# Two gathered tiles in one VectorE multiply, with one signal a pair, in the edge stages of a graph-attention kernel

## The chip, the cores and the metric

The kernel is one program on one core of a Trainium2 chip. The metric is the device time of one launch in microseconds (us). TensorE (PE), VectorE (DVE), ScalarE (ACT), GpSimd (POOL) and SyncE (SP) each run their own list of instructions and wait for one another through semaphores.

## The reference, cut to what matters

A node matrix x (6250 x 256) goes through two graph-attention layers, a mixing block and a mixture of experts. The change lies in the attention layers. There are 106,250 edges, sorted by their target node `dst`, and 8 heads of 32 columns:

```python
xp = (x @ W).reshape(-1, Hh, C)
alpha = leaky_relu(a_src[src] + a_dst[dst] + a_edge, 0.2)
m = segment_max(alpha, dst)
ex = exp(alpha - m[dst])
denom = segment_sum(ex, dst)
alpha = ex / (denom[dst] + 1e-16)
msg = xp[src] * alpha[:, :, None]
out = segment_sum(msg, dst)
```

## The kernel before, in words

The edges are cut into 832 tiles of 128 edges (one edge per partition), and these into 52 groups of GT = 16 tiles. `edges()` (line 591) runs once for each of the two layers, one after the other; each run is called an edge stage here. What the engines do for group g, tile k:

- **POOL** (`gather`, line 710): before tile k of group g+2 is fetched into `rows[q]`, it waits until the message of tile k of group g is made, which frees that slot (`s["msg"]`, line 715; the semaphore starts at 32). Then one indirect DMA (L717) fetches 128 rows of 1104 bytes.
- **DVE** (`step`, line 874): `message(g, q, k)` (L758) multiplies the 256 columns of a tile's rows by the 8 probabilities of each edge, which lie in PSUM (`ps_pr[q]`), writes `msg[:, k % 8]` and adds 1 to `s["msg"]`. It needs a free slot of 8: `total` of tile k-8. Between the messages of group g stand the steps of the softmax of group g+1 and the one-hot matrices: `one_hots` r=3 of group g+1 after message 1; r=0 of group g+2 after message 5; `leaky` (L777 to L782) after 6; `highest` (L788) after 7; `less_highest` (L793 to L796) after 8; `one_hots` r=1 after 9; `running` (L801) after 10; `whole` (L807 to L810) after 11; `inverse` (L814) after 12; `probability` (L821) after 13; `one_hots` r=2 after 14. In layer 0 `keys_centred` (L826) stands after message 10 and `keys_scales` (L831 to L835) after message 15; in layer 1 `mixed` (L847, L849) stands after message 15.
- `one_hots` r (L736/L737, then two L748) overwrites the one-hots of four tiles of group g, so that r=0 waits for `total` of tile 3, r=1 for that of tile 7 and r=2 for that of tile 11 (line 731).
- **PE** (`step`, line 1146): `total(k)` (L1101) waits for message k and for a free PSUM buffer of three, and multiplies message k by its one-hot matrix (four matmul records a tile). `scores` (L1074, L1083) r=3 of group g+1 follow total 2, r=0, 1, 2 of group g+2 follow totals 9, 10, 15; `turn_alpha` (L1090) follows total 6 and `turn_prob` (L1094) total 13. Layer 0 adds `key_sums` after total 4 and `keys` (L1110) after total 8, layer 1 `turn_squares` after total 0 and `mix` (L1139, L1142) after total 8.
- **ACT** (`window`, line 950): L955 and L956 take the sums of tile k out of PSUM and free the buffer for total k+3. In layer 0 `block_squares` (L993 to L998) follows window 11; it makes k2s, which `keys_scales` on DVE waits for. At each group's start ACT loads 16 registers.

The order on each engine is written out by hand; a loop body holds two groups (q = 0 and 1).

## Time and profile before

| | us |
|---|---|
| three runs | 3894.82, 3909.32, 3885.41; median 3894.82 |
| profiled execution, span from first to last instruction | 3896.2 |
| edge stage of layer 0, from its first message | 1533.4 |
| edge stage of layer 1, from its first message | 1448.4 |

The profiled execution's span, 3896.2 us, lies within the three runs and 1.4 us above their median. The four rows are told apart by where they come from: the first by timing, the others by the hardware profiler. In a row of the timeline the first number is the start, the second the time busy, "xN" how many instructions are merged, and the bracket the idle time of the engine before it with what ended it. A PE row says when PE took up an instruction, with a modelled end; when its semaphore arrived elsewhere is seen from those who waited.

### The profile page before, as it was taken

The page shows a single profiled execution, that of the slowest core. Times are in us where ns is not written, and L with a number is a line of the kernel's source. Part 1 is how long each engine was busy: PE and PEld are TensorE (multiplying, and loading weights), DVE is VectorE, ACT ScalarE, POOL GpSimd, SP SyncE. Part 2 cuts the span into 40 slices and gives each one's busy share as a digit, 9 for nine tenths or more (in the row PEclk, how much of TensorE's full clock was granted, in tenths as well). Part 3 has the DMA queues.
Part 4 walks back from the last instruction along what each step waited for, and adds up shares of the span by engine and source line. Part 5 has one row for each costly group of instructions (what it writes and reads, how often), then busy time and mean ns, then how long its engine had stood idle before and what let it go on. Part 6 is the DMA issues. An engine that isn't in the chain of part 4 may idle for free. (4 is left out here: it accounts for less than half of the span.)

```text
span 3896.2 us, 76131 instructions
## 1 busy us (share of the span) xinstructions
PE 2654.0 (68%) x15613; PEld 2243.8 (58%) x15614; DVE 2154.7 (55%) x6066; ACT 1173.1 (30%) x4747; POOL 2020.7 (52%) x2269
## 2 busy tenths in 40 slices
PE   6466677677676666684666666666666666659988
PEld 4355555556565555563555555555555556548877
DVE  6355555555554555561555555555555556675655
ACT  3133333333332333342222222222222223442222
POOL 3555455545455454436455555555555554635665
PEclk8677676776677777787677767777777767779999
DMA  9533343433333433314444444444444443454443
GB/s 252 144 112 110 109 122 111 115 112 113 107 111 110 116 111 107 108 52 125 114 118 129 117 127 121 118 131 117 131 115 127 124 116 94 143 151 149 152 119 97
DMA packets 282186, 473.15 MB, mean 121 GB/s; under 512 B 69124, under 2 KB 191644, under 8 KB 282116
## 3 DMA queue, kind: packets, MB, share of 16 engines
q0 software_dynamic: 96912, 288.68, 26.8%
q1 hardware_dynamic: 120884, 137.12, 12.0%
q10 hardware_dynamic: 64320, 46.56, 3.8%
q8 instruction: 27, 0.44, 0.0%
q14 instruction: 43, 0.35, 0.0%
HBM read 398.47 MB, written 75.78 MB: 122 GB/s over the span
## 5 line engine op out<-in xcount | busy, mean ns | idle before, releaser
L717 POOL DMA_INDIRECT e_rows<-table,e_idx x1664 | 1585.7, 953 | 1469.8 <-DVE e_msg L758 1006.6
L1101 PE MATMUL e_ps_sum<-e_hot,e_msg 128*128 128x129 f32 x6656 | 1456.5, 369 | 955.6 <-ACT parts L956 479.6
L1101 PEld LDWEIGHTS e_ps_sum<-e_hot,e_msg 128*128 128x128 f32 x6656 | 1209.5, 261 | 1142.1 <-ACT parts L956 622.2
L955 ACT ACTIVATE acc<-e_ps_sum 128x256 f32 x1664 | 640.5, 385 | 2094.7 <-remote 936.3
L737 DVE TENSOR_TENSOR e_hot<-e_ps_pr,rel 128x512 f32<-128x512 f32 x416 | 286.4, 689 | 932.4 <-PE e_ps_sum L1101 494.8
L758 DVE TENSOR_TENSOR e_msg<-e_rows,e_ps_pr 128x256 f32<-128x256 f32 x1664 | 655.3, 414 | 82.0 <-issue 9.9
L956 ACT ACTIVATE parts<-e_ps_sum 128x4 f32 (+1 forms) x1664 | 279.5, 168 | 0.0
L1083 PE MATMUL e_ps_al<-e_dst_score,e_hotT 128*128 x3328 | 249.0, 181 | 43.7 <-issue 42.4
L1083 PEld LDWEIGHTS e_ps_al<-e_dst_score,e_hotT 128*128 128x128 bf16 x3328 | 223.4, 104 | 87.3 <-issue 45.4
L748 DVE TENSOR_SCALAR e_hotT<-e_relb,pcolf 128x512 bf16<-128x512 bf16 x416 | 149.9, 360 | 52.2 <-remote 36.3
L2295 ACT ACTIVATE x_h<-x,eb 128x128 f32<-128x128 f32 x216 | 67.7, 364 | 271.4 <-PE x L2369 232.6
L748 DVE TENSOR_SCALAR e_hotT<-e_relb,pfar 128x512 bf16<-128x512 bf16 x416 | 147.2, 354 | 0.0
L788 DVE TENSOR_TENSOR_SCAN e_peak<-e_mark,e_ps_al 128x128 f32<-128x128 bf16 x104 | 43.7, 420 | 179.2 <-PE e_ps_al L1090 90.0
L2390 PE MATMUL x<-acc,x_h 128*128 x432 | 123.0, 408 | 18.9 <-DVE x_h L2325 13.7
L2369 PEld LDWEIGHTS x<-x_h,x_w 128*128 128x128 f32 x864 | 109.3, 194 | 28.4 <-ACT x_h L2295 15.7
L2369 PE MATMUL x<-x_h,x_w 128*128 128x128 f32 x864 | 122.2, 285 | 4.7 <-ACT x_h L2295 3.6
L2369 PE MATMUL x<-x_yT,x_w 128*128 128x128 f32 x864 | 116.7, 279 | 0.0
L2336 DVE TENSOR_TENSOR x_raw<-x,eb3b 128x256 f32<-128x256 f32 x108 | 45.9, 425 | 114.8 <-PE x L2390 93.8
L1110 PE MATMUL e_ps_a<-wkq,e_xT 128*128 128x512 f32 x200 | 108.0, 668 | 0.0
L2369 PEld LDWEIGHTS x<-x_yT,x_w 128*128 128x128 f32 x864 | 107.4, 195 | 0.1
L1118 PE MATMUL e_ps_b<-e_xc,e_k2r 128*128 128x256 f32 x200 | 101.8, 607 | 0.6 <-ACT e_k L1003 0.3
L814 DVE RECIPROCAL e_seg<-e_ps_pr 128x128 f32<-128x128 f32 x104 | 98.9, 951 | 0.1
(370 smaller groups left out, 3380.9 us busy)
## 6 DMA issues: line engine op xcount, KB each, us to landing
e_relb<-rel_rows SPq DMA_DIRECT2D x104, 512.0 KB
e_rows<-table,e_idx POOLq DMA_INDIRECT x1664
e_eattr<-in_edge_b SPq DMA_DIRECT2D x104, 128.0 KB
e_xT<-turned_x ACTq DMA_DIRECT2D x100, 128.0 KB
e_xr<-in_x ACTq DMA_DIRECT2D x100, 128.0 KB
node<-l_row SPq DMA_DIRECT2D x25, 512.0 KB, 3.1
table<-t_row SPq DMA_DIRECT2D x25, 276.0 KB
table<-j_row SPq DMA_DIRECT2D x25, 276.0 KB, 2.5
```

Source lines behind the costliest of these rows:

```text
L717: nc.gpsimd.indirect_dma_start(out=rows[q][:, k, :], out_offset=None, in_=table[0:NP], in_offset=bass.IndirectOffsetOnAxis(ap=idx[:, q, k: ...
L737: nc.vector.tensor_tensor(hot[:, q, 4 * r:4 * r + 4, 0:P], iota[c].unsqueeze(1).broadcast_to((P, 4, P)), rel[:, bass.ds(g * GT + 4 * r, 4) ...
L748: op = nc.vector.tensor_scalar(hotT[:, r % 2, far], relb[:, q, 4 * r:4 * r + 4, :], number[:, 0:1], None, ALU.is_equal)
L758: nc.vector.tensor_tensor(msg[:, k % RM, :].rearrange("p (h c) -> p h c", c=C), rows[q][:, k, 0:F].rearrange("p (h c) -> p h c", c=C), ps_ ...
L955: nc.scalar.activation(acc[:, :, bass.ds(at[k], P)], ps_sum[(k + q) % 3][:, :, 0:P], ACT.Copy).then_inc(s["window"], 1)
L956: nc.scalar.activation(parts[:, bass.ds(g * GT + k, 1)].rearrange("p t a b -> p (t a) b"), ps_sum[(k + q) % 3][:, :, 0:P + 1:P], ACT.Copy) ...
L1083: op = nc.tensor.matmul(parts_al[:, m, :], hotT[:, r % 2, far, k, :], pieces[:, bass.ds(b + far, 1), :].rearrange("p a c -> p (a c)"), sta ...
L1101: op = nc.tensor.matmul(ps_sum[(k + q) % 3][:, a, 0:WIN], msg[:, k % RM, a * P:a * P + P], hot[:, q, k, :], start=(a == 0), stop=True, ski ...
L1110: op = nc.tensor.matmul(ps_a[:], xT[:, q, a, :], wkq[:, a, :], start=(a == 0), stop=(a == 1))
L1118: nc.tensor.matmul(ps_b[:, a * F:a * F + F], k2r[:, a * P:a * P + P], xc[:], start=False, stop=False, skip_group_check=True)
L2369: op = nc.tensor.matmul(ps[k % 2][:, a * P:a * P + P], w[:, k % 2, m, h, a * P:a * P + P], of[:, h, :], start=(h == 0), stop=(h == 1))
L2390: op = nc.tensor.matmul(ps_3[k % 2][:, 0:F], h2[:, h, :], ew[:, 2, bass.ds(e, 1), h, :].rearrange("p e f -> p (e f)"), start=(h == 0), sto ...
```

## The change

DVE makes the messages of two tiles with one instruction (`messages(g, q, k)` for even k) of 128 x 512 elements, which waits for total k-7 and adds 1 to `s["msg"]` for the pair. POOL waits for the pair of its tile before each gather, PE before each even total. The softmax steps are placed between pairs: `one_hots` r=3 after pair 0, r=0 after pair 4, `leaky` after pair 6, `highest` and `less_highest` after pair 8, then after pair 10 `keys_centred` (layer 0), `one_hots` r=1 and `running`, after pair 12 `whole`, `inverse` and `probability`, and after pair 14 `keys_scales` (layer 0) or `mixed` (layer 1) and then `one_hots` r=2.

```diff
                 for k in range(GT):
-                    pool.wait_ge(s["msg"], 16 * g + k + 1)
+                    pool.wait_ge(s["msg"], 8 * g + k // 2 + 1)
                     pool.nop(nofuse=True)
...
-            def message(g, q, k):
+            def messages(g, q, k):
                 if k == 0:
                     vec.wait_ge(s["probT"], g + 1)
-                vec.wait_ge(s["sum"], 16 * g + 16 + k - RM + 1)
+                vec.wait_ge(s["sum"], 16 * g + 16 + k - RM + 2)
                 nc.vector.tensor_tensor(
-                    msg[:, k % RM, :].rearrange("p (h c) -> p h c", c=C),
-                    rows[q][:, k, 0:F].rearrange("p (h c) -> p h c", c=C),
-                    ps_pr[q][:, H * k:H * k + H].unsqueeze(2).broadcast_to((P, H, C)), ALU.mult).then_inc(s["msg"], 1)
+                    msg[:, k % RM:k % RM + 2, :].rearrange("p k (h c) -> p k h c", c=C),
+                    rows[q][:, k:k + 2, 0:F].rearrange("p k (h c) -> p k h c", c=C),
+                    ps_pr[q][:, H * k:H * k + 2 * H].rearrange("p (k h) -> p k h", k=2).unsqueeze(3).broadcast_to((P, 2, H, C)),
+                    ALU.mult).then_inc(s["msg"], 1)
...
-                for k in range(GT):
-                    message(g, q, k)
...
+                for k in range(0, GT, 2):
+                    messages(g, q, k)
+                    if softmax and k == 0:
                         one_hots(n, p, 3, None, q)
+                    if ahead and k == 4:
                         one_hots(g + 2, q, 0, i + 1, q)
                     if softmax and k == 6:
                         leaky(n, p, i if p == 1 else i + 1, more=ahead)
+                    if softmax and k == 8:
                         highest(n, p, i if p == 1 else i + 1)
                         less_highest(n, p)
+                    if block_too and layer == 0 and k == 10:
+                        keys_centred(g)
+                    if ahead and k == 10:
                         one_hots(g + 2, q, 1, i + 1, q)
                     if softmax and k == 10:
                         running(n, p)
+                    if softmax and k == 12:
                         whole(n, p)
                         inverse(p)
                         probability(n, p)
+                    if block_too and layer == 0 and k == 14:
+                        keys_scales(g)
+                    if block_too and layer == 1 and k == 14:
+                        mixed(g, q, i)
                     if ahead and k == 14:
                         one_hots(g + 2, q, 2, i + 1, q)
-            vec.sem_inc(s["msg"], 32)
+            vec.sem_inc(s["msg"], 16)
...
             def total(g, q, k):
-                pe.wait_ge(s["msg"], 16 * g + 32 + k + 1)
+                if k % 2 == 0:
+                    pe.wait_ge(s["msg"], 8 * g + 16 + k // 2 + 1)
```

## Rows read from the trace of the kernel before

**Rows 1.** Busy time by stage: window, busy us (instructions) by engine, PE clock, DMA share, GB/s
```profile
176.65:1710.06 1533.41, 1062.24 (x6050) 886.11 (x6049) 824.13 (x2452) 500.43 (x2214) 764.22 (x800) 0.72 0.39 110
1865.15:3313.57 1448.42, 948.48 (x5745) 825.00 (x5745) 819.69 (x2351) 391.45 (x1764) 760.47 (x800) 0.72 0.43 120
```

**Rows 2.** Groups by line, 1870 to 3310 us: busy, mean ns, idle before, releasers
```profile
L717 POOL DMA_INDIRECT e_rows<-table,e_idx x797 | 757.6, 951 | 663.5 <-DVE e_msg L758 460.0 <-issue 203.5
...
L758 DVE TENSOR_TENSOR e_msg<-e_rows,e_ps_pr 128x256 f32<-128x256 f32 x826 | 325.4, 414 | 39.8 <-remote 4.9 <-PE e_ps_sum L1101 2.1 <-issue 0.2
...
L737 DVE TENSOR_TENSOR e_hot<-e_ps_pr,rel 128x512 f32<-128x512 f32 x200 | 137.6, 688 | 496.9 <-remote 349.5 <-PE e_ps_sum L1101 147.4
```

**Rows 3.** Timeline of POOL in one group of layer 1
```profile
2492.46 0.94 POOL L717 DMA_INDIRECT e_rows<-table,e_idx  x1 [4.19 <-DVE e_msg L758]
2494.03 0.94 POOL L717 DMA_INDIRECT e_rows<-table,e_idx  x1 [0.62 <-issue]
...
2500.29 0.95 POOL L717 DMA_INDIRECT e_rows<-table,e_idx  x1 [0.30 <-issue]
2505.34 0.95 POOL L717 DMA_INDIRECT e_rows<-table,e_idx  x1 [4.11 <-DVE e_msg L758]
2507.06 0.95 POOL L717 DMA_INDIRECT e_rows<-table,e_idx  x1 [0.77 <-issue]
...
2516.07 0.95 POOL L717 DMA_INDIRECT e_rows<-table,e_idx  x1 [0.30 <-issue]
2521.28 0.95 POOL L717 DMA_INDIRECT e_rows<-table,e_idx  x1 [4.25 <-DVE e_msg L758]
```

**Rows 4.** Timeline of DVE in the same group
```profile
2492.82 0.75 DVE L758 TENSOR_TENSOR e_msg<-e_rows,e_ps_pr 128x256 f32<-128x256 f32 x2
...
2503.02 0.69 DVE L737 TENSOR_TENSOR e_hot<-e_ps_pr,rel 128x512 f32<-128x512 f32 x1 [6.62 <-PE e_ps_sum L1101]
...
2504.15 0.41 DVE L758 TENSOR_TENSOR e_msg<-e_rows,e_ps_pr 128x256 f32<-128x256 f32 x1
...
2514.16 0.41 DVE L758 TENSOR_TENSOR e_msg<-e_rows,e_ps_pr 128x256 f32<-128x256 f32 x1
2518.95 0.69 DVE L737 TENSOR_TENSOR e_hot<-e_ps_pr,rel 128x512 f32<-128x512 f32 x1 [4.38 <-remote]
...
2520.09 0.41 DVE L758 TENSOR_TENSOR e_msg<-e_rows,e_ps_pr 128x256 f32<-128x256 f32 x1
...
2521.41 0.74 DVE L758 TENSOR_TENSOR e_msg<-e_rows,e_ps_pr 128x256 f32<-128x256 f32 x2
```

**Rows 5.** Timeline of PE in the same group: total 3 and total 11
```profile
2496.88 0.71 PE L1101 MATMUL e_ps_sum<-e_hot,e_msg 128*128 128x129 f32 x4
...
2513.14 0.71 PE L1101 MATMUL e_ps_sum<-e_hot,e_msg 128*128 128x129 f32 x4
```

**Rows 6.** Timeline of DVE at the end of a group of layer 0
```profile
1005.67 0.41 DVE L758 TENSOR_TENSOR e_msg<-e_rows,e_ps_pr 128x256 f32<-128x256 f32 x1
1009.59 0.69 DVE L737 TENSOR_TENSOR e_hot<-e_ps_pr,rel 128x512 f32<-128x512 f32 x1 [3.51 <-PE e_ps_sum L1101]
...
1011.05 0.15 DVE L831 TENSOR_SCALAR e_k2s<-e_k2s 128x1 f32<-128x1 f32 x1
...
1012.18 0.75 DVE L758 TENSOR_TENSOR e_msg<-e_rows,e_ps_pr 128x256 f32<-128x256 f32 x2 [0.44 <-issue]
```

**Rows 7.** The same stretch on POOL (last gather of the burst) and on ACT
```profile
1007.56 0.95 POOL L717 DMA_INDIRECT e_rows<-table,e_idx  x1 [0.30 <-issue]
...
1010.21 0.20 ACT L993 ACTIVATION_READ_ACCUMULATOR e_k<-e_kq 128x1 f32 x1
```

**Rows 8.** Timeline of DVE in another group of layer 0
```profile
1302.70 0.42 DVE L788 TENSOR_TENSOR_SCAN e_peak<-e_mark,e_ps_al 128x128 f32<-128x128 bf16 x1 [3.71 <-PE e_ps_al L1090]
...
1306.99 0.69 DVE L826 TENSOR_TENSOR e_kq<-e_ps_a,bkq 128x512 f32<-128x512 f32 x1 [0.71 <-PE e_ps_a L1110]
...
1314.63 0.75 DVE L758 TENSOR_TENSOR e_msg<-e_rows,e_ps_pr 128x256 f32<-128x256 f32 x2 [0.44 <-issue]
```

More of the change, by code:

```diff
@@ L877, in step @@
                 block_too = not isinstance(g, int) or g < NB
-                for k in range(GT):
-                    message(g, q, k)
-                    if block_too and layer == 0:
-                        if k == 10:
-                            keys_centred(g)
-                        if k == 15:
-                            keys_scales(g)
-                    if block_too and layer == 1 and k == 15:
-                        mixed(g, q, i)
-                    if softmax and k == 1:
+                for k in range(0, GT, 2):
+                    messages(g, q, k)
+                    if softmax and k == 0:
                         one_hots(n, p, 3, None, q)
-                    if ahead and k == 5:
+                    if ahead and k == 4:
                         one_hots(g + 2, q, 0, i + 1, q)
@@ L892, in step @@
                         leaky(n, p, i if p == 1 else i + 1, more=ahead)
-                    if softmax and k == 7:
+                    if softmax and k == 8:
                         highest(n, p, i if p == 1 else i + 1)
-                    if softmax and k == 8:
                         less_highest(n, p)
-                    if ahead and k == 9:
+                    if block_too and layer == 0 and k == 10:
+                        keys_centred(g)
+                    if ahead and k == 10:
                         one_hots(g + 2, q, 1, i + 1, q)
@@ L900, in step @@
                         running(n, p)
-                    if softmax and k == 11:
+                    if softmax and k == 12:
                         whole(n, p)
-                    if softmax and k == 12:
                         inverse(p)
-                    if softmax and k == 13:
                         probability(n, p)
+                    if block_too and layer == 0 and k == 14:
+                        keys_scales(g)
+                    if block_too and layer == 1 and k == 14:
+                        mixed(g, q, i)
                     if ahead and k == 14:
                         one_hots(g + 2, q, 2, i + 1, q)
-            vec.sem_inc(s["msg"], 32)
+            vec.sem_inc(s["msg"], 16)
             vec.wait_ge(s_on, 1)
```

## The prediction

> **What bounds the kernel now.** I read the busy time by stage first. The two edge stages take 1533 and 1448 of the span's 3896.2 us, 77%, and in neither is an engine busy all the time: over the second, PE is busy 948 us, DVE 820 and POOL 760 of 1448 [rows 1]. So something passes the turn from one engine to another. The groups by line say where DVE stands still: not before its messages (40 us idle before 826 of them) but before the one-hots, 497 us before 200 [rows 2]. They wait for totals 3, 7 or 11, that is, for PE.
>
> Then I laid the timelines of one group of layer 1 beside each other. POOL's gathers come in bursts 1.25 us apart: gather 15 of the group before at 2492.46, gathers 0 to 5 from 2494.03 to 2500.29, idle, gathers 6 to 14 from 2505.34 to 2516.07, idle, gather 15 at 2521.28 [rows 3]. The one-hots r=0 run at 2503.02, r=2 at 2518.95, both after more than 4 us of idle time [rows 4]. But PE took up the totals that these wait for much earlier: total 3 at 2496.88 with an end at 2497.59, total 11 at 2513.14 with an end at 2513.85 [rows 5]. The reports come 5.4 and 5.1 us after these ends, and each comes shortly after a burst has ended: the last gather of the first burst ends at 2501.24 and the report is there 1.78 us later, the last of the second at 2517.02 and the report 1.93 us later. I read it so: while a burst of gathers runs, what PE has finished is reported late, and a group is a ring: burst, report, one-hots, message, next burst. In layer 0 the same is seen at the group's end: gather 14 ends at 1008.51, one-hots r=2 start at 1009.59 [rows 6, 7], 1.0 us later with the wait itself taken off.
>
> **A pair's price.** No row has a message of 128x512. Two messages back to back take 0.75 us, 0.34 from start to start [rows 4]. The nearest rows of 512 elements with an operand in PSUM are L737 with 688 ns [rows 2] and L826 with 690 [rows 8]. I take 0.69: a pair signals 0.28 us later than one message (0.414) did, and frees DVE 0.06 us sooner than two did. Bounds: 0.41 us (no more than now for one) and 0.83 (twice 0.414). With 8 pairs that is 0.5 us of DVE's time a group, which in layer 1 lies in the idle time before L737 and is worth nothing by itself. Half of the signals fall away; I price that at nothing, since no row shows idle time that a signal makes (0.2 us "issue" before 826 messages [rows 2]); the bounds are 0 and 0.05 us a pair.
>
> **Layer 1, by POOL's ring.** From gather 15 to the next gather 15 there are 28.82 us: 1.57 to gather 0, 6.26 to gather 5, 5.05 to gather 6, 1.72 to gather 7, 9.01 to gather 14, 5.21 to gather 15 [rows 3].
> - After the first burst: report, one-hots r=0 (1.13 us, from L737 at 2503.02 to the message at 2504.15), message, 0.78 us until POOL starts. With a pair 5.05 becomes 5.33.
> - Gathers 6 to 15: gather 7 no longer waits for `leaky`, which stood between messages 6 and 7, and gather 15 no longer for the report of total 11, because pair 14 makes message 15 before the one-hots r=2. DVE makes pair 14 at about the time of message 14 now (2514.16), and gather 14 is due at 2505.34 + 8 x 1.25 = 2515.3, so nine intervals of 1.25 to 1.26 follow: 11.3 us in place of 1.72 + 9.01 + 5.21 = 15.94.
> - After gather 15 comes what came after gather 14: 0.95 for the gather, 1.93 until the report, 1.13 for the one-hots r=2, 0.69 for pair 0, 0.78 until POOL starts: 5.48 in place of 1.57. `mixed` (1.0 us between 2520.4 and 2521.41) now lies before the one-hots, in the idle time before the report.
> - Sum: 5.48 + 6.26 + 5.33 + 11.3 = 28.37, 0.45 less than 28.82. Over some 50 groups: **-22 us**.
>
> So message 15 and `mixed` leave the path (1.33 us), but the report then comes one gather later. What is late next is the report itself, as before. The slot of a message is no new bound: pair k needs total k-7 where messages k and k+1 needed k-8 and k-7, and before L758 there are only 40 us of idle time in the whole stage [rows 2]. The steps that now stand behind a pair and not behind one message (`leaky` by 0.28 us) are covered by the 4.38 us that DVE waits at L737 later in the group [rows 4]; without that cover they would cost 0.28 each.
>
> A page of the Trainium skill speaks against reading the pauses so: "SBUF — State Buffer", section "SBUF: two separate sides", says that engine ports and DMA ports are disjoint and that PE never waits for anyone. The pauses in this trace end with the bursts all the same. What the rule would make of the change is the third rival.
>
> **Layer 0.** From the end of message 14 to the next message 0 there are 6.10 us (1006.08 to 1012.18): 3.51 waiting for total 11, 1.13 one-hots r=2, 0.33 message 15, 0.69 `keys_scales`, 0.44 the loop [rows 6]. After the change the order is pair 14, `keys_scales`, one-hots r=2. `keys_scales` waits for k2s, which ACT ends at 1010.41, 0.9 us after the report [rows 7]. Two cases:
> - *Total 11 is still reported after the burst.* The burst now ends with gather 15. From the end of pair 14: 0.78 to gather 14, 1.25 to gather 15, 0.95 for it, 1.0 to the report: 4.0; then 0.9 for k2s, 0.69, 1.13, 0.44: 7.17. The one-hots r=1 now stand behind L826 and not in front of its wait of 0.71 us [rows 8], so pair 14 ends some 0.3 us later (1.13 less the wait and less two messages' savings). Together **+1.4 us a group**.
> - *Total 11 is reported earlier.* Pair 8 no longer waits behind `highest` (which waited 3.71 us for PE [rows 8]), so gathers 6 to 9 and then 10, 11 come earlier, and there is a hole of about 2 us before pair 12, because the one-hots r=1 and `running` stand between. Through this hole the reports can pass. Then nothing is waited for behind pair 14: 0.69 + 1.13 + 0.44 = 2.26 in place of 6.10, less the 0.3: **-3.5 us a group**. The group at 1302.70 shows what such a group is like: DVE runs from L788 to the next message 0 in 11.9 us with 0.71 of waiting for PE in it [rows 8].
> I take 4 groups in 10 as free and 6 as held, as the trace of before has both sorts: 0.4 x (-3.5) + 0.6 x 1.4 = -0.56 a group, **-28 us** over 50. The ends are all held (+70) and, since a group that ends sooner meets its own next burst (pairs 4 and 6 need totals 13 and 15), not more than -2 us a group when all are free (-100).
>
> **Sum.** -22 - 28 = -50 from the profiled execution's 3896.2: **3846 us**. Its span lies 1.4 us above the median of the runs, less than their spread of 24, so nothing is added for that.
>
> **The rivals.**
> 1. *All of layer 0 is held* (slower). Place: `keys_scales` and one-hots r=2 behind pair 14, both behind one late report that now also waits for gather 15. Price +1.4 a group; it decides from the point at which more than 8 groups in 10 are held (there 0.8 x 1.4 = 1.12 stands against 0.2 x 3.5 + 0.45 = 1.15). For it: the wait of 3.51 us and the k2s that comes after it [rows 6, 7]. Against: the hole. 3896 + 70 - 22 = 3944.
> 2. *The hole lets nearly all reports through.* 3896 - 100 - 22 = 3774. For it: [rows 8]. Against: more groups back to back mean fewer idle stretches of POOL, through which PE catches up.
> 3. *The pauses are PE's own* and stay where they are, whatever POOL does (the page's rule). Then layer 1 gains all that stood behind the report, 2.46 - 1.13 = 1.33 a group [rows 4], -66, and layer 0 has 0.9 + 0.69 + 1.13 + 0.44 + 3.51 = 6.67 for 6.10, +28: 3896 - 38 = 3858.
> 4. *Only the later signal is felt.* The gathers do not close up, and at the two places a group where POOL stands idle for a message it gets a pair 0.28 us later: 0.56 x 102 groups = +57: 3953; half of it if the slack between gathers absorbs one place.
>
> **Chances.** A measurement of this kernel tells about 1% from no change, 39 us: faster is below 3857, slower above 3933. My forecast 0.38, of which 0.23 faster and 0.15 the same (its own range is 3810 to 3885). Rival 1 0.22: 0.18 slower, 0.04 the same. Rival 2 0.17, faster. Rival 3 0.12: 0.05 faster, 0.07 the same. Rival 4 0.11: 0.07 slower, 0.04 the same. Together faster 0.45, the same 0.30, slower 0.25. The range takes in both outer rivals and a little beyond: 3765 to 3965, which leaves out 2 in 10.
>
> **What would show it.** Right: 832 messages of 128x512 at about 0.69 us; in layer 1 ten gathers in a row from gather 6 on, and the one-hots r=2 starting 1.9 us behind the end of gather 15; stretches of 28.4 us from message 0 to message 0; `mixed` ahead of the one-hots r=2 and not behind a wait; in layer 0 a mixture of groups in which L831 waits and groups in which it does not. Wrong: a report of total 11 during the burst in layer 1, or at the old place (rival 3); L831 behind a wait of 4 us in nearly every group of layer 0 (rival 1) or in none (rival 2); gathers as far apart as before (rival 4); a pair far from 0.69 us.

## The result and the profile after

The changed kernel takes 3923.93 us (median of 8 runs, 3917.49 to 3949.38) against 3894.42 for the kernel before (8 runs beside them): a ratio of 1.0074 with an interval of 1.0055 to 1.0092, 0.7% slower. I had forecast 3846. The profiled execution is the slowest of the eight (3949.38, span 3947.6), so what the profile shows as lost, 51 us against the span of 3896.2, is more than the 30 us between the medians; the sizes by stage below are those of that one execution.

The costliest groups of the page of the kernel after (line, engine, operation; busy, mean ns; idle time before them and what ended most of it):

```profile
L717 POOL DMA_INDIRECT e_rows<-table,e_idx x1664 | 1577.1, 948 | 1524.1 <-DVE e_msg L758 1041.2
...
L737 DVE TENSOR_TENSOR e_hot<-e_ps_pr,rel 128x512 f32<-128x512 f32 x416 | 285.6, 687 | 766.4 <-PE e_ps_sum L1099 444.2
L758 DVE TENSOR_TENSOR e_msg<-e_rows,e_ps_pr 128x512 f32<-128x512 f32 x832 | 556.1, 679 | 74.4 <-PE e_ps_pr L1091 53.8
```

A pair takes 679 ns; 0.69 was forecast. And busy time by stage, to be read against [rows 1]:

```profile
174.32:1703.54 1529.22, 1053.48 (x6050) 886.00 (x6049) 789.14 (x2036) 500.67 (x2214) 759.48 (x800) 0.74 0.39 110
1858.42:3361.21 1502.79, 914.75 (x5745) 804.47 (x5744) 788.93 (x1935) 394.65 (x1764) 756.55 (x800) 0.75 0.41 116
```

Layer 0 is 4.2 us shorter, layer 1 is 54.4 us longer, 1.09 us a group. DVE works 35 and 31 us less in them, and that bought next to nothing. The whole loss lies in layer 1.

**Layer 1.** First DVE at the end of one group (start, us busy, what it is, and in brackets the idle time before it and what ended it), from pair 14 on:

```profile
2499.25 0.68 DVE L758 TENSOR_TENSOR e_msg<-e_rows,e_ps_pr 128x512 f32<-128x512 f32 x1
2501.40 0.43 DVE L848 TENSOR_TENSOR e_base<-e_ps_b,e_xr 128x256 f32<-128x256 f32 x1 [1.47 <-remote]
...
2506.18 0.69 DVE L737 TENSOR_TENSOR e_hot<-e_ps_pr,rel 128x512 f32<-128x512 f32 x1 [3.70 <-remote]
...
2508.75 0.69 DVE L758 TENSOR_TENSOR e_msg<-e_rows,e_ps_pr 128x512 f32<-128x512 f32 x1 [1.35 <-PE e_ps_pr L1091]
```

POOL in the same stretch, gathers 6 and 15 of the burst, and gather 0 of the next group:

```profile
2491.52 0.94 POOL L717 DMA_INDIRECT e_rows<-table,e_idx  x1 [3.95 <-DVE e_msg L758]
...
2502.77 0.95 POOL L717 DMA_INDIRECT e_rows<-table,e_idx  x1 [0.30 <-issue]
2510.21 0.95 POOL L717 DMA_INDIRECT e_rows<-table,e_idx  x1 [6.50 <-DVE e_msg L758]
```

ACT's first window after the burst, and the PE work that follows it:

```profile
2505.81 0.38 ACT L952 ACTIVATE acc<-e_ps_sum 128x256 f32 x1 [10.02 <-remote]
```

```profile
2506.31 2.09 PE L1099 MATMUL e_ps_sum<-e_hot,e_msg 128*128 128x129 f32 x8 [3.92 <-ACT parts L953]
2508.19 0.42 PE L1091 MATMUL e_ps_pr<-ident,e_prob 128*128 128x128 f32 x1
```

The gathers went as forecast: 6 to 15 in a row from 2491.52 to 2502.77, 11.25 us (so in 39 of the 50 groups; in the others the burst has a wait in it and takes 12.1 to 16.8). What came behind didn't. The report comes 2.46 us after the end of gather 15 (2503.72 to 2506.18), where 1.93 was forecast. Then DVE stands idle for 1.35 us before pair 0. Such a wait of over 0.5 us before message 0 stood in 3 groups of this layer before and stands in 43 now. Pair 0 needs `turn_prob` (L1091), and PE comes to that only behind totals 12 and 13 (the eight matmuls of 2506.31), which had themselves waited for ACT to empty a PSUM buffer. ACT had itself stood idle for 10.02 us before its first window. So a late report does not hold up DVE alone. It leaves a backlog on ACT and PE, and that is worked off only after it.

Before, this backlog was smaller. ACT's window 9 and PE's last work before message 0, in the group of [rows 4]:

```profile
2515.01 0.39 ACT L955 ACTIVATE acc<-e_ps_sum 128x256 f32 x1 [5.34 <-PE e_ps_sum L1101]
```

```profile
2519.28 1.23 PE L1101 MATMUL e_ps_sum<-e_hot,e_msg 128*128 128x129 f32 x4 [3.06 <-ACT parts L956]
2520.30 0.42 PE L1094 MATMUL e_ps_pr<-ident,e_prob 128*128 128x128 f32 x1
```

Window 9 ran inside the burst, 2.0 us before its end at 2517.02, and freed the buffer for total 12. So one total (13) stood between the report and `turn_prob`, which PE took up 1.35 us behind the one-hots r=2. After, window 9 runs only with the report (2505.81), two totals stand there, and it is 2.01 us. Over the groups 10 to 43 it is one total in 33 of 34 before and two in 29 of 34 after.

One group can mislead, so here is the ring of the prediction over the groups 10 to 43 of layer 1, worked out from the starts of the gathers, one-hots and messages in the traces (mean us a group; e9 and e10 are two kernels of the experiments below). "Last gather" is the last of the second burst: 14 before and in e9, 15 after and in e10.

| stretch | forecast | before | after | e9 | e10 |
|---|---|---|---|---|---|
| gather 6 to the last gather | 11.3 | 11.06 | 11.99 | 10.74 | 11.26 |
| last gather to one-hots r=2 | 2.88 | 2.64 | 3.04 | 2.96 | 2.98 |
| one-hots r=2 to the next gather 0 | 2.60 | 3.83 | 3.78 | 4.29 | 4.55 |
| of this, to message or pair 0 | 1.13 | 2.63 | 2.32 | 3.09 | 3.09 |
| gather 0 to gather 5 | 6.26 | 6.57 | 6.82 | 6.89 | 6.87 |
| gather 5 to gather 6 | 5.33 | 4.47 | 3.96 | 5.80 | 6.11 |
| whole group | 28.37 | 28.57 | 29.59 | 30.67 | 31.77 |

In most groups of the kernel after, the third row is 4.03 and the fourth 2.56 (the middle values); the means are lower because in some groups the report is not late.

**Layer 0.** The end of a group, DVE: `keys_centred` (L827), pair 12 (1309.03), pair 14, `keys_scales` (L832), one-hots r=2, and the next one-hots r=0:

```profile
1306.73 0.69 DVE L827 TENSOR_TENSOR e_kq<-e_ps_a,bkq 128x512 f32<-128x512 f32 x1 [1.99 <-issue]
...
1309.03 0.69 DVE L758 TENSOR_TENSOR e_msg<-e_rows,e_ps_pr 128x512 f32<-128x512 f32 x1 [0.15 <-issue]
...
1311.88 0.68 DVE L758 TENSOR_TENSOR e_msg<-e_rows,e_ps_pr 128x512 f32<-128x512 f32 x1
1312.48 0.15 DVE L832 TENSOR_SCALAR e_k2s<-e_k2s 128x1 f32<-128x1 f32 x1
...
1313.29 0.69 DVE L737 TENSOR_TENSOR e_hot<-e_ps_pr,rel 128x512 f32<-128x512 f32 x1
...
1326.99 0.69 DVE L737 TENSOR_TENSOR e_hot<-e_ps_pr,rel 128x512 f32<-128x512 f32 x1 [9.37 <-PE e_ps_sum L1099]
```

Behind pair 14 nothing waits any more: the free case of the forecast. But 9.37 us are lost at the next one-hots. To see how common this is, the waits before all one-hots of layer 0, first of the kernel before (68 + 16 + 1 waits in 50 groups), then of the kernel after (47 + 3):

```profile
its engine sat idle before it (us, times) until:
  PE e_ps_sum L1101: 347.4, 68
  remote: 83.0, 16
```

```profile
  PE e_ps_sum L1099: 363.6, 47
  remote: 21.4, 3
```

Before, there were nearly two late reports a group; after, there is one. But the time fell only from 431 to 391 us. And `keys_centred` now waits, first before, then after:

```profile
L826 DVE TENSOR_TENSOR e_kq<-e_ps_a,bkq 128x512 f32<-128x512 f32 x50 | 34.6, 692 | 23.2 <-PE e_ps_a L1110 16.2 <-issue 6.1
```

```profile
L827 DVE TENSOR_TENSOR e_kq<-e_ps_a,bkq 128x512 f32<-128x512 f32 x50 | 34.6, 691 | 140.2 <-remote 84.0 <-PE e_ps_a L1108 34.0 <-issue 22.2
```

That is 117 us more, against 39 gained before the one-hots, 31 before the messages (40.8 to 9.6) and 35 less of DVE's own work: these nearly cancel, and the stage is 4.2 us shorter. By one-hots, the 34 waits at r=2 are all gone; the 50 at r=0 stay and grow from 316 to 385 us.

### The profile page after: what moved, and what is told of

It reads as the page before. It is cut to its first block and busy times, and to the rows that moved or that the text cites. A ratio compares the mean times of both kernels' runs of the same rounds, so it can differ in the third digit from the quotient of the medians.

```text
span 3947.6 us, 72835 instructions
## 1 busy us (share of the span) xinstructions
PE 2608.1 (66%) x15613; PEld 2219.3 (56%) x15614; DVE 2088.3 (53%) x5234; ACT 1176.0 (30%) x4747; POOL 2011.0 (51%) x2269
## 5 line engine op out<-in xcount | busy, mean ns | idle before, releaser
L1099 PE MATMUL e_ps_sum<-e_hot,e_msg 128*128 128x129 f32 x6656 | 1348.9, 355 | 904.6 <-ACT parts L953 407.4
L1099 PEld LDWEIGHTS e_ps_sum<-e_hot,e_msg 128*128 128x128 f32 x6656 | 1161.4, 255 | 1022.4 <-ACT parts L953 602.7
L758 DVE TENSOR_TENSOR e_msg<-e_rows,e_ps_pr 128x512 f32<-128x512 f32 x832 | 556.1, 679 | 74.4 <-PE e_ps_pr L1091 53.8
L1080 PE MATMUL e_ps_al<-e_dst_score,e_hotT 128*128 x3328 | 296.1, 183 | 158.2 <-DVE e_hotT L748 80.7
L1080 PEld LDWEIGHTS e_ps_al<-e_dst_score,e_hotT 128*128 128x128 bf16 x3328 | 240.8, 102 | 234.1 <-issue 178.0
L2388 PE MATMUL x<-acc,x_h 128*128 x432 | 121.6, 404 | 21.5 <-DVE x_h L2323 14.7
L827 DVE TENSOR_TENSOR e_kq<-e_ps_a,bkq 128x512 f32<-128x512 f32 x50 | 34.6, 691 | 140.2 <-remote 84.0
```

The source lines that it names most:

```text
L758: nc.vector.tensor_tensor(msg[:, k % RM:k % RM + 2, :].rearrange("p k (h c) -> p k h c", c=C), rows[q][:, k:k + 2, 0:F].rearrange("p k (h ...
L1080: op = nc.tensor.matmul(parts_al[:, m, :], hotT[:, r % 2, far, k, :], pieces[:, bass.ds(b + far, 1), :].rearrange("p a c -> p (a c)"), sta ...
L1099: op = nc.tensor.matmul(ps_sum[(k + q) % 3][:, a, 0:WIN], msg[:, k % RM, a * P:a * P + P], hot[:, q, k, :], start=(a == 0), stop=True, ski ...
L2388: op = nc.tensor.matmul(ps_3[k % 2][:, 0:F], h2[:, h, :], ew[:, 2, bass.ds(e, 1), h, :].rearrange("p e f -> p (e f)"), start=(h == 0), sto ...
```

## The experiments

The kernels ran in five jobs, each beside the kernel before. In four of them the kernel before took 2979 to 2982 us, not 3894, and in one 3940. This was not foreseen, and it decides what each run can tell; I call the first sort *prompt* and the second *late*, as on the chip of the prediction. All ratios are to the kernel before in the same job.

### The prompt chips: the change moves nothing there

**e1** lets gather 15 wait for the next pair 0, which takes it out of the burst:

```diff
-                    pool.wait_ge(s["msg"], 8 * g + k // 2 + 1)
+                    pool.wait_ge(s["msg"], 8 * g + k // 2 + (1 if k < 15 else 2))
```

> The changed kernel, but POOL holds gather 15 of each group back until pair 0 of the next group (its rows are free earlier), so that the second burst ends with gather 14 as before the change. Theory A (what PE has finished is reported only after a burst has ended, and the change costs because gather 15 joined the second burst): in layer 1 the one-hots r=2 come about 1.25 us earlier than in the changed kernel, the mean group falls from 29.6 by 0.5 to 1.2 us, and the time falls by 25 to 60 us, to 3865 to 3900. Rival B (the pair's first signal, 0.28 us later, costs): nothing changes in the ring but a gather moved, the time stays at 3910 to 3940. Rival C (the pauses are PE's own): the same as B, and the one-hots r=2 stay where they are.

**e2** brings `turn_prob` forward from behind total 13 to behind total 11:

```diff
-                    if softmax and k == 13:
+                    if softmax and k == 11:
```

> The changed kernel with turn_prob on PE after total 11 and not after total 13. In the changed kernel pair 0 of the next group starts 2.1 us after the one-hots r=2 in layer 1 and not 1.13, since it waits for the turned probabilities, which stand on PE behind total 13 and so behind window 10, that is behind the late report. Theory A (that wait is a term of its own on the path): pair 0 follows the one-hots at once, the group of layer 1 falls by 0.7 to 1.0 us, the time by 25 to 50 us, to 3875 to 3900. Rival D (POOL's ring and the report set the pace, the wait is covered by them): within 10 us of the changed kernel.

**e3** keeps the new order but makes two single messages with a signal each:

```diff
                 for k in range(0, GT, 2):
-                    messages(g, q, k)
+                    message(g, q, k)
+                    message(g, q, k + 1)
...
```

The waits of POOL and PE count by tile again, as in the kernel before.

> The changed kernel's order of steps, but with two single instructions and two signals in place of each pair (832 pairs become 1664 messages). Theory A (the order costs, since messages 14 and 15 are made before the late report, and the pair instruction is worth little): within 12 us of the changed kernel, 3912 to 3936. Rival B (the pair's late first signal costs 0.28 us at two places a group): 30 us or more faster than the changed kernel. A third view, that the pair instruction saves time on DVE's path: 15 us or more slower than the changed kernel.

**e4** has pairs in nearly the old order: `highest` behind pair 6, the one-hots r=1 behind pair 8, `whole` behind pair 10, and the one-hots r=2 ahead of pair 14, so that gathers 14 and 15 wait for the report:

```diff
                 for k in range(0, GT, 2):
+                    if ahead and k == 14:
+                        one_hots(g + 2, q, 2, i + 1, q)
                     messages(g, q, k)
...
                     if softmax and k == 6:
                         leaky(n, p, i if p == 1 else i + 1, more=ahead)
+                        highest(n, p, i if p == 1 else i + 1)
                     if softmax and k == 8:
-                        highest(n, p, i if p == 1 else i + 1)
                         less_highest(n, p)
+                    if ahead and k == 8:
+                        one_hots(g + 2, q, 1, i + 1, q)
...
                         running(n, p)
-                    if softmax and k == 12:
                         whole(n, p)
+                    if softmax and k == 12:
                         inverse(p)
...
-                    if ahead and k == 14:
-                        one_hots(g + 2, q, 2, i + 1, q)
```

> Pairs as in the changed kernel, but the steps stand as near to their old places as pairs allow: highest before pair 8, one-hots r=1 after pair 8 and before keys_centred, whole after pair 10, and one-hots r=2 before pair 14, so that gathers 14 and 15 both wait for the report of total 11. Theory A (the order around the report is what costs): the second burst ends with gather 13, the report comes 1.25 us earlier than before the change and about 2.5 us earlier than in the changed kernel, but two gathers then run in the next burst. The time is 3870 to 3905, near the kernel before. Rival B (the pair costs wherever it stands): 3925 or more.

Measured beside 2978.98 us before: e1 2978.49 (0.9990, interval 0.9975 to 1.0004), e2 2978.40 (0.9989, 0.9974 to 1.0003), e3 2974.55 (0.9988, 0.9973 to 1.0002), e4 2978.65 (0.9994, 0.9984 to 1.0004). All four theories missed, since the kernel before itself was another: to see why, **e5** is the kernel before and **e6** the kernel after, unchanged.

> The kernel before, unchanged, for its profile on a chip of the experiments, where it took 2979 us beside the first four kernels and not 3894. Theory A2 (on the chip of the two first profiles PE's reports come late while gathers run, on this chip they come at once, and then POOL's 1664 gathers 1.25 us apart bound the edge stages): 2970 to 2990 us, gathers 1.25 us apart with little idle time, the one-hots r=0 and r=2 within 1 us of the end of totals 3 and 11. Rival (this chip is faster in the instructions or transfers themselves): gathers, messages or matmuls are shorter than in the first profile. If the chip is of the first kind, 3880 to 3910 and the first profile again.

> The changed kernel, unchanged. Theory A2 (POOL's gathers bound the stages where the reports come at once, and the change moves no gather there): within 0.3% of the kernel before, if that takes 2979. Rival (the pair saves DVE's time on the path): 0.5% or more faster. If the kernel before takes 3894 here: 0.5 to 0.9% slower, as in the first result.

e5 2978.38 us (one execution); e6 2977.23 (0.9993, 0.9983 to 1.0003). The page of e5, the kernel before on a prompt chip:

```profile
L717 POOL DMA_INDIRECT e_rows<-table,e_idx x1664 | 1582.4, 951 | 561.0 <-issue 399.2
...
L758 DVE TENSOR_TENSOR e_msg<-e_rows,e_ps_pr 128x256 f32<-128x256 f32 x1664 | 653.5, 413 | 74.6 <-PE e_ps_sum L1101 10.3
L737 DVE TENSOR_TENSOR e_hot<-e_ps_pr,rel 128x512 f32<-128x512 f32 x416 | 285.1, 685 | 157.7 <-PE e_ps_sum L1101 152.4
```

One gather, one message and one set of one-hots last as long as on the late chip. What is gone is the waiting: the gathers have 561 us idle before them where they had 1470 on the page of before, most of it "issue", in other words POOL's own step from one gather to the next, and the one-hots wait 158 us. The timeline of POOL shows gathers 1.25 us apart all through a group, 16 of them in 20.02 us:

```profile
1979.56 0.94 POOL L717 DMA_INDIRECT e_rows<-table,e_idx  x1 [0.30 <-DVE e_msg L758]
...
1999.58 0.95 POOL L717 DMA_INDIRECT e_rows<-table,e_idx  x1 [0.30 <-issue]
```

A group takes 20.6 us there on average. So where reports are prompt, POOL's gathers are nearly all of a group's time, and what DVE does is hidden. **e7** and **e8** take that cover away: they leave out the gathers of the odd tiles, in the kernel before and in the kernel after (the output then lacks those rows' share; `leaky` waits for 8 landed gathers a group in place of 16).

```diff
+                    if k % 2 == 0:
                         nc.gpsimd.indirect_dma_start(
...
```

> The kernel before with the gathers of odd tiles left out (their rows stay zero), so that POOL has 8 gathers a group in place of 16. Theory A2: where the kernel before takes 2979, POOL no longer bounds and the next bound (the ring of DVE, PE and ACT) shows: a group falls from 20.4 us by 0.5 to 3 us. Where it takes 3894, the pauses before the one-hots shrink with the bursts, and the group falls from 28.6 and 30.2 us by 6 us or more. Rival (PE's late reports have nothing to do with gathers): where it takes 3894, the pauses stay as long as they were.

> The changed kernel with the same gathers left out. With POOL out of the way this shows what pairs and the new order are worth to DVE, PE and ACT alone. My estimate from the two profiles: 0.5 us a group less on DVE, against turn_prob's wait before pair 0 and the later scales, so within 1% of the half-gather version of the kernel before. Rival (the pair instruction is a gain that the gathers hide): 1.5% or more faster than that one. Rival (the order is a loss by itself): 1.5% or more slower.

e7 2802.41 us (0.9404, 0.9388 to 0.9419), e8 2814.76 (0.9445, 0.9429 to 0.9461): with POOL half idle the change costs 0.4%. By stage it isn't one effect but two. Over the groups 10 to 43 of layer 1 the messages 0 stand 18.73 us apart in e7 and the pairs 0 18.05 in e8, 0.68 less; in layer 0 19.06 and 19.91, 0.85 more. The one-hots in layer 0 (160 to 1120 us), e7 first:

```profile
L738 DVE TENSOR_TENSOR e_hot<-e_ps_pr,rel 128x512 f32<-128x512 f32 x199 | 136.2, 685 | 74.1 <-PE e_ps_sum L1103 74.1
```

```profile
L738 DVE TENSOR_TENSOR e_hot<-e_ps_pr,rel 128x512 f32<-128x512 f32 x192 | 131.5, 685 | 131.7 <-PE e_ps_sum L1101 125.7
```

In layer 1 the granted clock of TensorE is nearly the same in the two (0.93 and 0.94), and the kernel after gains there: DVE's time counts where POOL doesn't. In layer 0 it loses more, at the one-hots and at `keys_centred` (2.7 us of waiting in e7, 32.5 in e8), which both wait for PE. But the granted clock of layer 0 also differs, 0.98 in e7 and 0.88 in e8, and PE is busy for 854.72 and 902.81 us. How much of the 0.85 is the order and how much the slower PE, no run separates.

### Late reports rebuilt on a prompt chip

**e9** is the kernel before with late reports put in by hand: DVE's one-hots r=0 and r=2, and ACT's windows 2 and 9, also wait until gathers 0 to 5, or 0 to 14, of group g+2 have landed.

```diff
                     vec.wait_ge(s["sum"], 16 * g + 4 * r - 12)
+                    if r in (0, 2):
+                        vec.wait_ge(s[f"rows{q}"], 256 * i + 16 * (6 if r == 0 else 15))
...
+                    if k in (2, 9) and (not isinstance(g, int) or g + 2 < NG):
+                        act.wait_ge(s[f"rows{q}"], 256 * i + 256 + 16 * (6 if k == 2 else 15))
```

> The kernel before with the late reports rebuilt by hand: where the first profile showed them late, VectorE (one-hots r=0, r=2) and ScalarE (windows 2 and 9) wait until the data of the first 6 and the first 15 gathers of group g+2 have landed, which are the gathers of the two bursts. Nothing is left out. Theory A3 (a report that comes when the burst has ended is what made a group 28.6 us long, and nothing else of that chip is needed): a group of layer 1 takes 27.5 to 29.5 us, with two bursts and two idle stretches of POOL of about 4 us, and the time is 3700 to 3950 us. Rival (that chip is slow for another reason, this does not rebuild it): under 3400.

**e10** is the kernel after with the same waits; the second is for gathers 0 to 15, since gather 15 is part of its burst (16 for 15 in both lines).

> The changed kernel with the same waits; the second burst now has gather 15 in it, so that the second wait is for all 16 gathers of group g+2. Theory A3: the second report comes one gather (1.25 us) later, pair 0 then waits for turn_prob behind total 13 and window 10, and a group of layer 1 is 0.5 to 1.5 us longer than in the kernel before with the same waits; the time is 0.5 to 2.5% more than that one's. My old step (the ring without the turn_prob term): 0.4 us a group less than that one. Rival: no difference within 0.3%.

e9 4115.69 us (1.3813 of before), e10 4228.10 (1.4199), beside 2980.5. The rule was put in by hand, so that the report comes one gather later in e10 is assumed, not shown. What is shown is whether the kernel after gains elsewhere what this costs. It doesn't. The two edge stages, e9 and then e10:

```profile
155.29:1839.53 1684.24, 1049.78 (x6050) 858.96 (x6049) 830.58 (x2452) 503.95 (x2215) 763.74 (x806) 0.73 0.35 100
1972.37:3535.85 1563.48, 940.07 (x5743) 818.52 (x5742) 816.31 (x2351) 390.87 (x1764) 763.04 (x806) 0.72 0.40 112
```

```profile
153.35:1889.59 1736.24, 1043.27 (x6048) 861.52 (x6048) 796.38 (x2036) 504.31 (x2214) 763.51 (x806) 0.75 0.34 97
2021.20:3639.30 1618.10, 895.90 (x5743) 802.21 (x5742) 785.74 (x1935) 391.12 (x1764) 762.22 (x806) 0.72 0.38 108
```

Layer 1 grows by 54.6 us, as in the real pair (54.4). Layer 0 grows by 52, where the real pair lost nothing: here the rebuilt rule is too strict, as it holds the one-hots r=2 in every group. So e9 and e10 stand for layer 1 alone. Even there 54.6 beside 54.4 is in part chance: the profiled execution of the kernel after was 25 us above its median. And e9 holds ACT's window 9 until the report, which the real kernel before did not, so that two totals stand ahead of `turn_prob` in all of its groups. That makes the pair a clean test of the other half: what taking DVE's work away is worth once PE's backlog is the same. Message 0 behind the one-hots r=2, in e9 (message 15 and `mixed` between them) and in e10 (nothing between them):

```profile
2710.23 0.69 DVE L739 TENSOR_TENSOR e_hot<-e_ps_pr,rel 128x512 f32<-128x512 f32 x1 [4.46 <-issue]
...
2713.30 0.75 DVE L760 TENSOR_TENSOR e_msg<-e_rows,e_ps_pr 128x256 f32<-128x256 f32 x2 [0.55 <-PE e_ps_pr L1098]
```

```profile
2722.31 0.69 DVE L739 TENSOR_TENSOR e_hot<-e_ps_pr,rel 128x512 f32<-128x512 f32 x1 [4.81 <-DMA e_rows<-table,e_idx]
2725.38 0.69 DVE L760 TENSOR_TENSOR e_msg<-e_rows,e_ps_pr 128x512 f32<-128x512 f32 x1 [1.86 <-PE e_ps_pr L1095]
```

It is 3.07 us in both. The 1.33 us of DVE's work that the change took away stands in the second as idle time: `turn_prob` is what both wait for. The table above says where the 1.10 us between e9 and e10 arise: 0.52 in the burst, which has gather 15 more and a wait for `leaky` less; 0.26 between pair 0 and gather 0, and 0.31 up to gather 6, the two places at which POOL waits for a message and a pair signals later than one message did.

**e11** (e10 with `turn_prob` behind total 11, the edit of e2) and **e12** (e10 with gather 15 held back, the edit of e1, and the second wait for 15 gathers again) take the two suspects one at a time.

> As the changed kernel with late reports, with turn_prob after total 11 in place of 13, in front of the window that is late. Theory A3 (the wait of pair 0 for the turned probabilities is a term of its own): pair 0 follows the one-hots r=2 at once, 0.7 to 1.0 us a group less than the changed kernel with late reports, 70 to 100 us in all. Rival D (POOL's ring covers that wait): within 15 us of it.

> As the changed kernel with late reports, with gather 15 held back until pair 0 of the next group, and the second wait for 15 gathers as in the kernel before. Theory A3: the second report comes 1.25 us earlier, but gather 15 then leads the next burst and ends the first burst 1.25 us later, as before the change; a group is 0.2 to 0.9 us shorter than in the changed kernel with late reports. Rival B (the pair's later signal is the cost): no shorter.

e11 4215.72 us (1.4152), e12 4188.97 (1.4055). In e11 pair 0 no longer waits for `turn_prob` and starts 1.13 us behind the one-hots r=2 instead of 3.1, but the pair of tiles 2 and 3 then starts 4.7 us after pair 0 instead of 3.0: the one-hots r=3 ahead of it overwrite those of tiles 12 to 15, and so wait for total 15, the end of PE's backlog (2.8 us of idle time where e10 has 1.0). Of 1.9 us only 0.38 a group are kept in layer 1 (1599.05 for 1618.10), and layer 0 gives 0.25 of that back. The backlog is one piece, and the next wait behind it pays. In e12 layer 1 takes 1586.11: holding gather 15 back returns 0.64 of the 1.09 us a group. It isn't the kernel before in this place, though: gather 15 now waits for pair 0 and delays gather 0 by 1.25 us (5.80 us from the one-hots r=2), so that what the second burst gains is lost again, and what remains is gained in the next burst.

### A late chip

The next job met a late chip: 3940.13 us before (3928.47 to 3953.89). The three kernels that ran on it carry the rebuilt waits besides the chip's own late reports, so they are all longer, and they can be compared with one another only.

**e13** is e10 with the single messages of e3, **e14** e10 in the order of e4 (second wait for 14 gathers, the last before the report), **e15** e10 with the one-hots r=2 directly behind pair 14:

```diff
                     messages(g, q, k)
+                    if ahead and k == 14:
+                        one_hots(g + 2, q, 2, i + 1, q)
```

> The kernel after with the late reports rebuilt (e10), but each pair is again two single messages with a signal each; the order of the softmax steps is the new one. Theory (the new order costs: gather 15 joins the burst, the report is a gather later, and the backlog of PE and ScalarE behind it is bare; the pair itself costs next to nothing): within 0.5% of e10's 4228 us, so 4207 to 4249, and layer 1 again 1.0 to 1.2 us a group longer than in e9. Rival (the pair's later signal is what is felt, 0.28 us at two places a group): 0.56 x 102 = 57 us less than e10, 4171, and if the signal is all of the loss, e9's 4116.

> Pairs, but the order of before as far as pairs allow it: highest after pair 8, then the one-hots r=1, and the one-hots r=2 ahead of pair 14, so that gathers 14 and 15 wait for the report, as gather 15 did before; rebuilt late reports: the second one until gather 13 has landed (the last that doesn't depend on it). Theory (order costs, pair is free): the report comes one gather (1.25 us) earlier than in e9 and two earlier than in e10, but two gathers stand behind it instead of one: in layer 1 near e9, 4070 to 4160 us in all. Rival (the pair's signal is felt): as e10, 4200 or more.

> e10 with one line moved: the one-hots r=2 stand directly behind pair 14, ahead of keys_scales (layer 0) and mixed (layer 1). Theory for layer 0 (its loss of 1.06 us a group against e9 is made behind the report: keys_scales, 0.69 us, waits for k2s and holds up the one-hots r=2 and with them PE's first scores): 0.5 to 1 us a group less in layer 0, and nothing in layer 1, where pair 0 waits for probT anyway: 4175 to 4205 us. Rival (layer 0 too is bound by PE's and ScalarE's backlog behind the report): within 0.4% of e10, 4211 to 4245.

e13 4361.38 us (1.1059, 1.1015 to 1.1102), e14 4232.05 (1.0731, 1.0691 to 1.0772), e15 4341.23 (1.1017, 1.0974 to 1.1060). The times expected for them by the theories were worked out from prompt chips and all missed; e14 lies in its rival's range (4200 or more), which on this chip says nothing. The stages tell more. Layer 0 and layer 1 of e13, then of e14, then of e15:

```profile
174.62:1942.22 1767.60, 1065.20 (x6050) 882.79 (x6049) 824.19 (x2452) 515.86 (x2214) 758.03 (x800) 0.72 0.34 95
2097.11:3763.12 1666.01, 938.78 (x5745) 826.85 (x5744) 817.24 (x2351) 401.05 (x1763) 758.68 (x800) 0.71 0.37 105
```

```profile
176.44:1907.78 1731.34, 1062.68 (x6050) 906.37 (x6049) 806.70 (x2036) 500.54 (x2214) 758.26 (x800) 0.69 0.34 97
2061.32:3639.34 1578.02, 961.37 (x5744) 848.23 (x5744) 792.07 (x1935) 391.87 (x1764) 758.37 (x800) 0.70 0.39 111
```

```profile
176.02:1922.16 1746.14, 1039.76 (x6050) 858.18 (x6049) 800.75 (x2036) 513.62 (x2214) 759.06 (x800) 0.73 0.34 96
2075.55:3741.41 1665.86, 931.13 (x5745) 817.39 (x5745) 786.54 (x1935) 395.44 (x1763) 758.42 (x800) 0.71 0.37 105
```

e13 and e15 have the same layer 1 within 0.2 us. That looks like proof that single messages or pairs make no difference. It isn't. The waits of DVE in the stage, e13 and then e15 (the one-hots, and `running`):

```profile
L739 DVE TENSOR_TENSOR e_hot<-e_ps_pr,rel 128x512 f32<-128x512 f32 x201 | 138.6, 689 | 495.5 <-DMA e_rows<-table,e_idx 323.4 <-remote 110.7 <-issue 48.4
...
L807 DVE TENSOR_TENSOR_SCAN e_ps_pr<-e_mark,e_ps_pr 128x128 f32<-128x128 bf16 x51 | 21.8, 427 | 121.4 <-ACT e_ps_pr L950 64.1 <-issue 57.2
```

```profile
L739 DVE TENSOR_TENSOR e_hot<-e_ps_pr,rel 128x512 f32<-128x512 f32 x201 | 138.6, 690 | 741.2 <-PE e_ps_sum L1103 266.5 <-DMA e_rows<-table,e_idx 240.1 <-issue 208.3
...
L804 DVE TENSOR_TENSOR_SCAN e_ps_pr<-e_mark,e_ps_pr 128x128 f32<-128x128 bf16 x51 | 21.8, 428 | 21.4 <-issue 21.4
```

In e13 `running` waits 100 us more, in the middle of the second burst, which takes 13.36 us a group where e15 has 11.45; in e15 the gap between gathers 5 and 6 is 7.03 where e13 has 5.43, and gather 0 comes 0.35 later. The parts differ by up to 1.9 us a group and happen to cancel. They differ in the place of `mixed` too. So what the pair's later signal costs on a late chip stays open. e14 and e15 both have pairs and differ in the order and in the gather that the report follows: 87.8 us in layer 1, 1.76 us a group, in favour of the old order. In layer 0 e15 is 21.5 us shorter than e13, 0.43 a group, just under the lower end of what was expected for taking `keys_scales` from in front of the one-hots r=2; since the pair changed with it, that share is not settled.

### Once more without rebuilt waits

**e16**, **e17** and **e18** are e3, e4 and the kernel after, unchanged, once more in case they meet a late chip.

> The kernel of e3 once more: the new order of the steps with single messages, no wait added. The case hangs on which kind of chip it meets. Where the kernel before takes about 2980 us (reports at once) it says nothing new: within 0.3% of before. Where before takes about 3900 us or more (late reports): theory (the new order costs, the pair is free) 0.4 to 1.2% slower than before, as the kernel after; rival (the pair's later signal costs) within 0.3% of before.

> The kernel of e4 once more: pairs, but the one-hots r=1 after pair 8 and the one-hots r=2 ahead of pair 14, no wait added. Where the kernel before takes about 2980 us: within 0.3% of it. Where it takes about 3900 us or more: theory (the order costs) for layer 1: 1.25 from gather 15 to gather 0, 6.26, 5.33, seven intervals of 1.25 to gather 13 (8.78), then 0.95 + 1.93 + 1.13 + 0.69 + 0.78 = 5.48 to gather 14, 1.25 to gather 15, together 28.35 us a group against 28.6 before and 29.6 after; PE's scores follow the one-hots r=2 beside gathers 14 and 15. In all 0.98 to 1.00 of before. Rival (the pair costs): 1.004 to 1.012.

> The kernel after once more beside the two others, so that all four mixtures of order and pair stand on one chip. Where the kernel before takes about 2980 us: within 0.3% of it, as in e6. Where it takes about 3900 us or more: 1.004 to 1.011, as first measured (1.0074).

The job met a prompt one (2982.19 us): e16 2980.47 (0.9987, 0.9975 to 0.9998), e17 2982.70 (0.9996, 0.9983 to 1.0010), e18 2977.73 (0.9980, 0.9967 to 0.9992). The kernel after is at most 0.3% faster there, and nothing was learned of a late chip. Whether pairs in the old order beat the kernel before on a late chip stays open: e14 sets them only against the new order, and with rebuilt waits.

## Why the prediction was wrong

- **The pair's price**, 0.69 us: measured 0.679. Right. That fewer signals are worth nothing was priced without a run that separates it, and none here does.
- **The gathers 6 to 15 in one burst**, 11.3 us: 11.25 in 39 of 50 groups, 11.99 on average. Right in the main, and so was `mixed` ahead of the one-hots.
- **"The report then comes one gather later", 1.93 us behind the burst's end**: it did, and 2.5 us behind it in most groups. Why 0.6 later is not shown.
- **"1.13 for the one-hots r=2, 0.69 for pair 0, 0.78 until POOL starts", 2.60 us: this is the step that failed.** From the one-hots r=2 to gather 0 it took 4.03 us (2506.18 to 2510.21), 3.78 on average; before, it had been 3.83. I had booked message 15 and `mixed`, 1.33 us, as work on the path that could be taken off it. But DVE was never alone there: beside it PE works off its totals and `turn_prob`, and message 0 can't start before. By the rows of before, message 0 followed `turn_prob` by 1.1 us and could have done so by 0.56, as pair 0 does after: about half a microsecond was to be had at best (my estimate), not 1.33. And the change took that away too, since the unbroken burst left total 12 in the backlog, so that `turn_prob` comes 0.66 us later. Gather 15 had been free: it ran between the one-hots r=2 and gather 0. Now it stands in front of the report, 1.25 us.
- **The sum of layer 1**, 28.37 a group, measured 29.59, so 1.22 too little. By the table: 1.18 for the failed step, 0.69 for bursts with a wait in them, 0.56 between gathers 0 and 5 and 0.16 for the report, less 1.37 between gathers 5 and 6, where the first report is often not late. The base was off as well: the group that I took has 28.82 us, the average is 28.57, so that against the average my sum was worth 0.20 a group and not 0.45: 10 us and not 22.
- **Layer 0, -28 us**: measured -4.2. I took 4 groups in 10 as free behind pair 14, and 47 of 50 were. What failed is the price of -3.5 for a free group. The next burst starts right behind the last one, in the group shown the gathers run from 1313.32 to 1322.29 without a break, and the report that was no longer late at the group's end is late by 9.37 us at the one-hots r=0. The rest went at `keys_centred`: I had counted with its wait of 0.71 us [rows 8] and let nothing grow, but it grew by 2.3 us a group (23.2 to 140.2 us). It now stands ahead of the one-hots r=1, and PE's part for it isn't ready. The sentence against rival 2 names the first half of this; I left its price out of the sum. This account rests on the two traces alone: no experiment moved `keys_centred` back by itself.
- **The rivals.** Rival 1 (all held) fell: the reports behind pair 14 came in time. Rival 2 was right about the hole and wrong about its worth. Rival 3, that the pauses are PE's own and keep their place, stood on the Trainium skill, "SBUF — State Buffer", section "SBUF: two separate sides". On the late chip the report moved with the burst, one gather later, which speaks against it there; e5 shows no such pauses with the same gathers, so on the prompt chips nothing contradicts the page. What holds a report back is not shown by any run. Rival 4 (only the signal is felt) named the right sign, but its condition failed: the gathers did close up. A later signal is in the loss all the same, 0.26 us at each of two places between e9 and e10; my sum had it in.

What is shown: in the real traces the loss lies in layer 1, the second burst is longer by 0.93 us a group and the way from the one-hots r=2 to gather 0 is no shorter (3.83 and 3.78), with one total more ahead of `turn_prob`. With rebuilt late reports message 0 comes 3.07 us behind the one-hots r=2 with DVE's work there or without it (e9, e10), and taking its wait away mostly moves the wait to the next place (e11). Only assumed is that the real report follows the burst's last gather, as the rebuilt one does by hand; in the real traces it comes 1.9 us behind that gather's end before and 2.5 after, in the middle. Only argued is why window 9 now waits for the report (the burst has lost its short waits). Open is how the real 1.09 us divides between gather 15, the larger backlog, the pair's later signal and a report that comes 0.6 us later behind the burst.

## What to carry to other kernels

Work that stands behind a late event is on the path only if no other engine has a backlog from the same event; before taking it off, follow each engine that the event releases to the next point where they meet. Don't let an engine run on into the stretch that makes the event late: a transfer that was hidden behind the event is not hidden ahead of it. And take a period from all groups of a stage, not from one, before claiming half a microsecond of it.

## What the runs showed of the hardware

The same kernel takes 3894 and 3940 us in two jobs and 2979 to 2982 in four. The instructions last the same (a gather 953 and 951 ns, a message 414 and 413), and the gathers stand 1.25 us apart in both. Two things differ. PE's reports during a burst of gathers come late in the one sort and at once or nearly so in the other: the one-hots' idle time is 932 us on the page before and 158 in e5. And the granted clock in the edge stages is 0.72 [rows 1] there, and here 0.95 and 0.89:

```profile
152.98:1209.57 1056.59, 867.94 (x6049) 699.50 (x6048) 823.25 (x2452) 498.98 (x2214) 767.10 (x807) 0.95 0.57 160
1343.68:2399.21 1055.53, 807.61 (x5743) 686.75 (x5742) 813.61 (x2351) 391.13 (x1764) 765.69 (x806) 0.89 0.58 166
```

Both are means over stretches at TensorE's two levels, 2.4 and 1.2 GHz. The low clock alone does not make reports late. e9 has 0.73 and 0.72 on a prompt chip, and there the one-hots of layer 1 wait for the landing put in by hand or for nothing that the profile names, and for PE in none of the waits:

```profile
L739 DVE TENSOR_TENSOR e_hot<-e_ps_pr,rel 128x512 f32<-128x512 f32 x200 | 137.9, 689 | 593.5 <-DMA e_rows<-table,e_idx 302.6 <-issue 290.9
```

On the late chip the reports of totals 3 and 11 came only after the burst in the groups shown; that of total 9, for window 9, came inside it (2515.01, 3.2 us behind PE's end of that total at 2511.80), so a report is late during a burst but not always held to its end. Whether this belongs to the chip or to its state at the time wasn't tried. A forecast from one trace holds for that kind alone: on the prompt kind POOL's gathers are nearly all of a group, 16 x 1.25 of 20.6 us, and the kernel after takes 0.998 to 0.9993 of the time.
